# A Mamba-and-attention image kernel: projection weights padded to the full array, and half of its transfers issued from inside the scan

## The reference, cut to what matters

```python
xs = jnp.concatenate([x_hwwh, jnp.flip(x_hwwh, axis=-1)], axis=1)   # row order, column order, both reversed
x_dbl = jnp.einsum('bkdl,kcd->bkcl', xs, x_proj_w)                  # 192 channels -> 6 + 16 + 16 rows
dts, Bs, Cs = jnp.split(x_dbl, [DT_RANK, DT_RANK + D_STATE], axis=2)
dts = jnp.einsum('bkrl,kdr->bkdl', dts, dt_w)
# step: h = exp(d_t * A) * h + (d_t * u_t) * b_t ;  y = sum over n of h * c_t   (16 states n, 4096 positions)
```

## Time and profile before

| what | value |
|---|---|
| median of 3 runs | 15098.41 us (15097.98 to 15100.52) |
| profiled execution, its time | 15108.91 us |
| its span in the trace | 15107.2 us |
| VectorE busy | 12257.9 us, 81% |
| TensorE busy | 11199.9 us, 74%, mean granted clock 0.84 |
| POOL busy | 9980.3 us, 66% |
| ScalarE busy | 6850.2 us, 45% |

### The profile page before, as it was taken

One profiled execution on the slowest core, in us unless ns is written; L12 is line 12 of the kernel. 1 busy time (PEld: TensorE's weight loads), 2 busy tenths in 40 slices (PEclk: granted clock), 3 DMA queues, 4 the chain that ended last, 5 costly groups with the idle time before them and its releaser, 6 DMA issues. The chain is left out here.

```text
span 15107.2 us, 97020 instructions
## 1 busy us (share of the span) xinstructions
PE 11199.9 (74%) x24688; PEld 4335.5 (29%) x24688; DVE 12257.9 (81%) x8679; ACT 6850.2 (45%) x10234; POOL 9980.3 (66%) x4293
## 2 busy tenths in 40 slices
PE   6777877778777787777877778777787777877777
PEld 2222322223222232222322223222222222222222
DVE  5999569995699956999569995699956999569995
ACT  3444444444444444444444444444444444444444
POOL 2898338983389833898238982389823898238982
PEclk8888878888788887888878888788887888878888
DMA  3676336763367633676336763367633676336763
GB/s 103 201 205 201 90 93 202 206 201 88 97 201 206 200 87 100 200 206 200 84 103 200 206 200 82 103 200 207 200 81 105 199 208 201 78 107 199 207 201 76
DMA packets 692726, 2391.49 MB, mean 158 GB/s; under 512 B 136576, under 2 KB 136576, under 8 KB 682752
## 3 DMA queue, kind: packets, MB, share of 16 engines
q1 hardware_dynamic: 688672, 2362.35, 53.4%
q10 hardware_dynamic: 3456, 22.55, 0.8%
HBM read 2300.09 MB, written 67.11 MB: 157 GB/s over the span
## 5 line engine op out<-in xcount | busy, mean ns | idle before, releaser
L1019 POOL TENSOR_TENSOR state<-state,c_sb 128x1024 f32<-128x1024 f32 x3072 | 7190.9, 2356 | 1101.2 <-ACT carry L834 1099.2
L797 PE MATMUL ps<-state,wt 128*128 128x512 f32 x12288 | 6666.4, 684 | 1135.2 <-DVE ya L945 629.3
L797 PEld LDWEIGHTS ps<-state,wt 128*128 128x128 f32 x12288 | 2724.2, 224 | 4103.2 <-issue 2524.5
L1008 POOL TENSOR_TENSOR dbu<-b_sb,du 128x1024 f32<-128x1024 f32 x1152 | 2710.8, 2353 | 1237.0 <-DVE du L992 1237.0
L975 DVE TENSOR_TENSOR_SCAN state<-decay,carry,ps 128x1024 f32<-128x1024 f32 x1440 | 3379.6, 2347 | 51.3
L834 ACT COPY carry<-state 128x1 f32<-128x1 f32 x3072 | 588.4, 192 | 5734.9 <-DVE state L975 5725.8
L775 PE MATMUL ps<-parts,sel 114*128 114x512 bf16 x3840 | 1387.7, 449 | 1863.1 <-DVE state L975 1857.4
L962 DVE TENSOR_TENSOR ps<-ps,du 128x1024 f32<-128x1024 f32 x1920 | 2328.8, 1213 | 411.2 <-PE ps L775 410.3
L875 ACT ACTIVATE decay<-delta,a_neg 128x1024 f32<-128x1024 f32 x1920 | 2195.2, 1144 | 6.2
L975 DVE TENSOR_TENSOR_SCAN state<-ps,carry,dbu 128x1024 f32<-128x1024 f32 x864 | 2015.9, 2333 | 0.0
L875 ACT ACTIVATE ps<-delta,a_neg 128x1024 f32<-128x1024 f32 x1152 | 1278.0, 1109 | 0.0
(11 more groups left out here) (178 smaller groups left out, 10381.8 us busy)
## 6 DMA issues: line engine op xcount, KB each, us to landing
c_sb<-bc SPq DMA_DIRECT2D x2048, 512.0 KB, 4.3
c_sb<-bc SPq DMA_DIRECT2D x2048, 256.0 KB, 4.7
b_sb<-bc SPq DMA_DIRECT2D x768, 512.0 KB, 4.8
b_sb<-bc SPq DMA_DIRECT2D x768, 256.0 KB, 5.3
x_nat<-x SPq DMA_DIRECT2D x17, 1536.0 KB, 9.2
gates<-gate_a SPq DMA_DIRECT2D x8, 2048.0 KB, 6.4
bc<-xf ACTq DMA_DIRECT2D x64, 256.0 KB, 6.8
gate_a<-gates SPq DMA_DIRECT2D x8, 2048.0 KB, 9.7
```

What stands on the lines that cost most here:

```text
L797: mm = pe.matmul(py[:, q * CH:(q + 1) * CH], col("ident"), state[:, slot(g, n), q * CH:(q + 1) * CH], start=(n == 0), stop=(n == NS - 1))
L1008: pool.tensor_tensor(dbu[:, i % BRING, :], b_sb[:, i % BRING, :], du[:, :], ALU.mult)\
L1019: pool.tensor_tensor(state[:, slot(g, n), :], state[:, slot(g, n), :], c_sb[:, n % CRING, :], ALU.mult).then_inc(S["weighted"], 1)
```

## The change

The projection's weights `w_xp` become four blocks of 128 x 128 that hold zeros where there were no weights: the matmul over `ur` now uses all 128 partitions (the other order's half meets zero rows) and writes 128 PSUM rows instead of 96. All transfers of `prep_b` are issued by SyncE. Those of row order go out as their pieces are complete; of column order only the first half of the B and C rows is stored before the barrier. The other half of those rows (4 transfers) and all its copies into `parts` (12 transfers) are issued by `late(i)`, two ahead of each C load of the first eight states of the scan's first chunk. So that pass T = 0 does not touch the rows that are still under way, its `spread` uses partitions 0 to 47 and its `pre_dt` partitions 96 to 113. Waits for the late ones stand before the second pass's loads (SP), before its step sizes (PE) and before the first `take_y` (DVE), whose output tiles lie over the pieces. ScalarE waits for the stored gates only before column order.

```diff
-    w_xp = put("w_xp", [128, 3, XROWS], F32)
+    w_xp = put("w_xp", [128, 4, 128], F32)
...
                     sp.wait_ge(S["parts_zero"], 2)
-                    for o in range(2):
-                        stack(sp, o, 0, hi, S["xp_rest"])
-                        stack(sp, o, 2, lo, S["xp_low"])
+                    sp.wait_ge(S["xp_hi"], NCH)
+                    for g in range(2):
+                        to_parts(sp, 0, 0, g, hi).then_inc(S["parts_in"], 16)
+                        to_parts_dt(sp, 0, 0, g, hi).then_inc(S["parts_in"], 16)
...
+                    sp.wait_ge(S["xp_out"], NCH + NCH // 2)
+                    for g in range(2):
+                        for kind in range(2):
+                            to_rows(sp, 1, 0, g, kind).then_inc(S["bc_stored"], 16)
                     sp.wait_ge(S["gates_stored"], 32)
-                    sp.wait_ge(S["gn_stored"], 16)
                     sp.wait_ge(S["bc_stored"], 8 * 16)
-                    sp.wait_ge(S["parts_in"], 24 * 16)
+                    sp.wait_ge(S["parts_in"], 12 * 16)
...
-                        out_ = xp_bank[i % (2 * SLOTS)][0:XROWS, :]
+                        out_ = xp_bank[i % (2 * SLOTS)]
...
-                        half = slice(DR * o, DR * o + DR)
-                        pe.matmul(out_, w_xp[half, 2, :], ur[half, sl(j)], start=False, stop=True)\
+                        pe.matmul(out_, w_xp[:, 2 + o, :], ur[:, sl(j)], start=False, stop=True)\
...
-                    act.wait_ge(S["gates_stored"], 32)
-                    act.wait_ge(S["gn_stored"], 16)
...
+                        if i == NCH:
+                            act.wait_ge(S["gates_stored"], 32)
...
+                        if T == 0 and following[0] == 1:
+                            sp.wait_ge(S["bc_stored"], 12 * 16)
                         for n in range(NS):
+                            if g * NS + n < LATE // 2:
+                                late(2 * n)
+                                late(2 * n + 1)
...
+                        own = slice(0, 3 * NS) if T == 0 else slice(0, XR3)
...
+                        own = slice(6 * NS, XR3) if T == 0 else slice(0, XR3)
...
+                                if g == NSC - 1:
+                                    pe.wait_ge(S["parts_in"], 24 * 16)
...
+                        if g == 0:
+                            dve.wait_ge(S["parts_in"], 24 * 16)
+                            dve.wait_ge(S["bc_stored"], 12 * 16)
```

More of the change, by code:

```diff
@@ L34 @@
 DT0, C_ROW, XROWS = 2 * NS, 4 * NS, 6 * NS
+PIECE = DT0 + 2 * RANK
+LATE = 16
 GROUPS = 32
@@ L533, in _, with to_parts, to_parts_dt, to_rows @@
                               (4, in_proj))
+        def to_parts(eng, o, p, g, piece):
+            return eng.dma_start(parts[(3 * o + p) * NS:(3 * o + p + 1) * NS, 2 * g, :],
+                                 piece[o][NS * g:NS * g + NS, :])
+        def to_parts_dt(eng, o, p, g, piece):
+            return eng.dma_start(parts[6 * NS + p * RANK:6 * NS + (p + 1) * RANK, 2 * g + o, :],
+                                 piece[o][DT0 + RANK * g:DT0 + RANK * g + RANK, :])
+        def to_rows(eng, o, part, g, kind):
+            row = NS * g if kind == 0 else C_ROW + NS * g
+            if o == 0:
+                return eng.dma_start(bc_dram[2 * g + kind, 0], xf_nat[row:row + NS, :])
+            return eng.dma_start(bc_dram[2 * g + kind, 1, :, part * (L // 2):(part + 1) * (L // 2)],
+                                 xf_col[part][row:row + NS, :])
         def prep_b():
             xp_bank = [ps[2 + i // SLOTS][i % SLOTS] for i in range(2 * SLOTS)]
[L539 to L546, removed]
             with nc.Block() as block:
@@ L643, in _ @@
                             middle(i - 1)
[L644 to L650, removed]
-                            if o == 0:
-                                act.wait_ge(S["parts_zero"], 2)
-                            stack(act, o, 1, mid, S["xp_mid"])
                 @block.vector
@@ L756, in steps, with late @@
                                          POOLED.index(n + B_AHEAD - NS))
+                    def late(i):
+                        if i < 4:
+                            to_rows(sp, 1, 1, i // 2, i % 2).then_inc(S["bc_stored"], 16)
+                        else:
+                            p = (i - 4) // 4
+                            which = to_parts if i % 2 == 0 else to_parts_dt
+                            which(sp, 1, p, i // 2 % 2, (hi, mid, low)[p]).then_inc(S["parts_in"], 16)
                     def spread_b(T, at, g, i):
@@ L785, in pre_dt @@
                                 for p in range(3):
-                                    mm = pe.matmul(pc[:, q * CH:(q + 1) * CH], dt_w[:, p, w, :],
-                                                   part_cols(at, k, q), start=(i == 0 and p == 0),
+                                    mm = pe.matmul(pc[:, q * CH:(q + 1) * CH], dt_w[own, p, w, :],
+                                                   part_cols(at, k, q, own), start=(i == 0 and p == 0),
                                                    stop=(i == len(ways) - 1 and p == 2))
```

47 lines of the change are left out of this document (31 added, 16 removed).

## The result

| | before | after |
|---|---|---|
| median of 6 runs each, us | 15098.19 | 14746.02 |
| lowest to highest, us | 15094.95 to 15106.67 | 14740.69 to 14751.86 |
| profiled execution: time and span, us | 15108.91, 15107.2 | 14743.57, 14741.9 |
| mean granted clock | 0.84 | 0.858 |

The ratio is 0.9766 (95%: 0.9753 to 0.9779): 352 us less, 44.0 an image, where 318 and 39.75 were forecast.

What follows compares the result with a forecast made beforehand. VectorE was taken to bound the scan and TensorE at 1.2 GHz the projection, which lies on the path with the gap. 15108.9 - 328 + 10 = 14791 us profiled, 14780 against the median; range 14745 to 14880.

Steps and rivals of the forecast that it cites:

- What bounds the kernel; projection and gap on the path: VectorE limits the scan, TensorE at 1.2 GHz the projection; projection and following gap, 82 us an image, lie on the path.
- Part 1, the projection: Padded weights let TensorE's clock rise after three matmuls, ending the projection at 213.6 instead of 239.45: 25.8 us less.
- Part 2, the transfers: Between projection and scan: one queue issues in 14.0 plus 3.5 us, and the scan starts at 218.5 instead of 259.6.
- Part 3, "Paid: 1.25 us an image, 10 in eight": In pass 0 of the scan: 0.75 us for three spread waits and 0.5 for a later clock rise, an image.
- The sum: 15108.9 - 328 + 10 = 14791 us for the profiled execution, 14780 against the median of the runs.
- the term of 41 us an image: Saving from the shorter projection and gap together, before the scan's start: 328 us in eight images.
- quite hidden: Fast-edge condition for the transfers between projection and scan: 42.5 us an image saved, toward 14745.
- still warm: Other fast-edge condition: TensorE's clock has not fallen when the scan starts; no size of its own was given.
- Slow queue: Rival: one queue needs 26.7 us for column order's 16 transfers' issues; 31.3 us an image saved, 14858; chance 0.12.
- Clock stays at 1.2 GHz: Rival: in the projection only the alternation's cost goes; 23.9 us an image saved, 14917; chance 0.08.
- The paying scan: Rival: late transfers delay C or B loads in the scan by 10.6 us an image; 14865; chance 0.08.
- Pass 0 becomes TensorE's: Rival: smaller matmuls keep the clock down, chunks take 70.5 us against 57; 104 us slower, 15202; chance 0.03.

Runs made afterwards that it cites:

- e1_rows: Kernel before, with the matmul over `ur` widened to all 128 partitions by zero weights, still 96 columns: 14937.1 us, ratio 0.9897.
- e2_cols: Kernel before, with 128 weight columns in both projection matmuls and the 64-partition matmul kept: 15098.9 us, ratio 1.0004.
- e9_all64: Kernel before, with every projection matmul on partitions 0 to 63, so its output differs: 15043.4 us, ratio 0.9964.
- e5_own: Kernel before, with only pass 0 of the scan limited to 48 partitions for spreads and 18 for `pre_dt`: 15089.9 us, ratio 0.9995.
- e7_y3: Changed kernel with `Y_AT` = 3 instead of 4, so VectorE takes each finished sum one state earlier: 14378.0 us, ratio 0.9522.
- e11_before_y3: Kernel before with `Y_AT` = 3 instead of 4 alone, the sum taken one state earlier: 14683.2 us, ratio 0.9725.
- e10_double: Changed kernel with each of the 16 late transfers issued twice, the second into spare memory: 14772.3 us, ratio 0.9783.
- e8_straight: Changed kernel with column order's matmul over `ua` reading without a stride, so its output differs: 14740.9 us, ratio 0.9762.
- e6_all_before: Changed kernel with all 16 late transfers put back ahead of the barrier, on SyncE's queue: 14858.2 us, ratio 0.9841.
- e4_late: Changed kernel with the old 96-column and 64-partition matmuls, so the moved transfers and pass 0's limits alone: 14961.5 us, ratio 0.9912.
- e3_pad: Kernel before with the full padding to 128 x 128 weights alone, transfers as before: 14941.4 us, ratio 0.9900.

## Why the prediction was nearly right, and where it was off

- **What bounds the kernel; projection and gap on the path**: held. They became shorter by 340 us, and the time fell by at least as much.
- **Part 1, the projection**: held. Forecast 25.8 us less, measured 26.14. "I take a rise after three matmuls, 5.1 us" was too long, since the clock rose after two, 3.3 us; 0.86 for a matmul and 1.70 for a strided one stood as read from `post_a` and the convolution. The early rise is partly offset by column order, which took 20.8 us and not 20.4. Why the clock rises was argued there from shape alone; e1_rows, e2_cols and e9_all64 show that the matmuls of 64 partitions had kept it down.
- **Part 2, the transfers**: the mechanism held, the sizes not quite. Counted from the projection's start (177.0 in the forecast, 174.8 now): one queue took 15.5 us for row order's 16 transfers (190.93 to 206.43), not 14.0, but began at 16.1 instead of 16.8, since row order's matmuls were done 0.9 us earlier, at 15.3 instead of 16.2. The column half took 3.06 and not 3.5, so the issues ended at 34.7 (forecast 34.3). They had landed by 39.7, where 40.2 was forecast from 6.8 us for a landing. The last piece was ready at 39.3 (39.8), and the barrier after it took 0.47 us, not "1 us for the barrier". So the scan starts at 39.7 and not at 41.5: what was mis-sized here is the step from the last piece to the scan, 1.7 us in the forecast (39.8 to 41.5).
- **Part 3, "Paid: 1.25 us an image, 10 in eight"**: this step failed, in its mechanism. No time was paid: e5_own, which has this part alone, came to 0.9995 of the kernel before, and the changed kernel's scan takes 1377.3 us against 1378.6. Small operands do keep the clock down in pass 0, as the prediction feared, and TensorE is busy for 12.3 us an image more. The step from there to the time was wrong: it let VectorE wait longer by what TensorE loses, but TensorE stood idle for VectorE anyway, up to 5.86 us a chunk, and the cost went into that idle time; VectorE's own waits stayed (50.6 against 51.6 us). The prediction had the 5.86 us in its rows and did not ask whether they would take the cost in. With most of them removed the price shows, about 3.3 us an image (e7_y3 against e11_before_y3).
- **The sum**: 34 us more saved than forecast. 12 of them are projection and gap: the term of 41 us an image was too small and measured 42.49. 10 are the payment that was not made. 12 are left, 1.5 an image; the prediction had the rest of the kernel at no change, the runs show it 1.6 us an image shorter, which is inside the spread of like kernels, and the cause stays open. The range's fast edge, 14745, is 353 us below the median of before. 340 of these are the 42.5 us an image for the transfers "quite hidden", which is what came; for the other 13, for a TensorE "still warm" at the scan's start, the prediction has no working. The first six `pre_dt` matmuls did take 1.99 us and not 2.72, but that is 6 us in eight images. So that the time came to lie on this edge is in part luck.
- **Rivals.** Slow queue: it needed 26.7 us, and 15.5 came. Clock stays at 1.2 GHz: true of e9_all64 and e2_cols, not of the change. The paying scan: not at this size, true at twice (e10_double). Pass 0 becomes TensorE's: its chunks last as long as before; its mechanism, small operands that keep the clock down, is real, for part of a chunk.

## What to carry to other kernels

Look at TensorE's granted clock stage by stage; a stretch that is busy throughout at 0.50 and has matmuls of 64 partitions may be lifted by zero rows that fill the partitions, as e1_rows did with 128 x 96 weights, at no cost in time. Then ask which engine must keep up at twice the pace: here ScalarE, which issued transfers between its copies, held back more than a quarter of the projection's gain until they were moved. And before adding a small cost, look for idle time of the same engine ahead of the point where others need it: it may take the cost in. The cost will then show only when that idle time is removed, which here was worth more than the change itself.

## What the runs showed of the hardware

- Idle time and the clock: in the changed kernel, after a gap of 3.71 us, the first six `pre_dt` matmuls took 1.99 us; after 8.83 (e8_straight) and 16.98 us (e6_all_before) the same six, with the same 18 partitions, took 2.71. In e4_late, whose projection ran at 1.2 GHz, they took 2.71 also after 3.71 us. So the clock was still up after the short gap, and fell during the six.
- Alternating 128 and 64 partitions cost 0.22 us per fp32 matmul at 1.2 GHz (before against e9_all64), but more columns cost too: the 128-column matmuls of e2_cols took 2.00 us each where 96 columns took 1.95, at the same clock.
- Eight transfer issues held ScalarE for 11.32 us (e3_pad), while SyncE issued the other eight; in the changed kernel SyncE alone issued the same sixteen in 15.5. So the second queue won little and stopped an engine that had other work.
